# Deeper rings for the attention probabilities in a latent-attention and feed-forward layer, with a new hand-written order

## The reference

```
x = x + layernorm(attention(layernorm(x)))
x = x + layernorm(ffn(layernorm(x)))
```

## Time and profile before

| | us |
|---|---|
| median of 3 runs | 1710.68 (1709.68 to 1716.02) |
| the profiled execution, its own time | 1718.1 |
| its span, first to last instruction | 1716.3 |
| TensorE / VectorE / ScalarE / GpSimd busy | 1572.2 / 1147.7 / 1069.0 / 952.9 |
| DMA queue q1, share of 16 engines | 72.0% |
| mean granted TensorE clock | 0.980 |

### The profile page before, as it was taken

The page is one execution under the profiler, slowest core; times in us unless marked ns, Lnnn a source line. Parts: engine busy times, 40 slices in busy tenths (PEclk is TensorE's granted clock), DMA queues, the critical chain, the costliest instruction groups (busy, mean ns, idle before and its releaser), DMA issues.

```text
span 1716.3 us, 30452 instructions
## 1 busy us (share of the span) xinstructions
PE 1572.2 (92%) x10720; PEld 1275.9 (74%) x10720; DVE 1147.7 (67%) x2548; ACT 1069.0 (62%) x2159; POOL 952.9 (56%) x911
## 2 busy tenths in 40 slices
PE   5878999999998999998999999999978899999997
PEld 5856777778777777777877777777766677888775
DVE  6866677777777777776777777777766542323356
ACT  5677777777777777777877777777754433212122
POOL 2556677677676677676767677677622321111132
PEclk9899999999999999999999999999998999999998
DMA  8669999998999989899889898988996300201022
GB/s 280 227 140 206 164 200 181 189 200 174 203 175 190 180 190 201 184 187 188 171 172 190 164 179 169 183 171 165 184 186 239 121 25 1 74 1 39 1 92 80
DMA packets 661095, 268.84 MB, mean 157 GB/s; under 512 B 608432, under 2 KB 619184, under 8 KB 658768
## 3 DMA queue, kind: packets, MB, share of 16 engines
q1 hardware_dynamic: 660944, 266.90, 72.0%
HBM read 69.70 MB, written 29.36 MB: 58 GB/s over the span
## 4 chain that ended last, share of the span: by engine, by line
PE 56%; DMA 14%; DVE 11%; ACT 6%; POOL 6%; issue 4%; SPq 2%; POOLq 0%; ACTq 0%; DVEq 0%
PE f_ps L116 14%; PE s_ps L973 12%; PE x_ps L116 11%; DMA pt<-pk 10%; PE o_ps L987 9%; PE fd_ps L116 6%; DMA qs<-q_raw 3%; DVE pk L1384 3%; PE x_ps L996 2%; DVE s_ps L1371 1%; POOL q_low L1561 1%; POOL qf L1554 1%; POOL qs L1551 1%; SPq L772 1%; ACT ot_high L1194 1%
## 5 line engine op out<-in xcount | busy, mean ns | idle before, releaser
L1384 DVE SCALAR_TENSOR_TENSOR pk<-s_ps,pk 128x256 f16<-128x256 f32 (+7 forms) x512 | 383.7, 749 | 132.7 <-ACT pk L1176 132.4
L1168 ACT ACTIVATE s_ps<-s_ps,nbias 128x256 f32<-128x256 f32 (+7 forms) x512 | 371.3, 725 | 129.7 <-DVE nbias L1371 126.2
L1371 DVE CUSTOM_DVE_ANT_0 s_ps<-s_ps,far_sb 128x256 f32<-128x256 f32 (+7 forms) x512 | 388.4, 759 | 36.1 <-PE s_ps L973 30.9
L987 PEld LDWEIGHTS o_ps<-lat,pt 128*128 128x128 f16 x4608 | 268.2, 98 | 137.7 <-issue 70.4
L1176 ACT ACTIVATE pk<-s_ps 128x256 f16<-128x256 f32 (+7 forms) x512 | 339.6, 663 | 34.1 <-DMA pt<-pk 28.4
L987 PE MATMUL o_ps<-lat,pt 128*128 128x130 f16 x4608 | 312.0, 221 | 51.6 <-DMA pt<-pk 41.9
L1551 POOL TENSOR_TENSOR qs<-qs,sin_q 64x512 f32<-64x512 f32 x128 | 164.4, 1284 | 224.7 <-DMA qs<-q_raw 217.9
L973 PE MATMUL s_ps<-k_high,q_high 128*128 128x512 f32 (+3 forms) x768 | 283.6, 369 | 5.0 <-DVE k_low L1351 2.0
L973 PE MATMUL s_ps<-k_low,q_high 128*128 128x512 f32 (+3 forms) x768 | 257.1, 347 | 0.0
L1599 POOL TENSOR_TENSOR mid_low<-mid,mid_high 128x512 fp32r<-128x512 f32 (+1 forms) x44 | 57.2, 1300 | 303.1 <-ACT mid_high L1265 303.1
L973 PE MATMUL s_ps<-k_high,q_low 128*128 128x512 f32 (+3 forms) x768 | 224.3, 346 | 0.0
(11 more groups left out here) (134 smaller groups left out, 2622.1 us busy)
## 6 DMA issues: line engine op xcount, KB each, us to landing
weff_in<-weff SPq DMA_DIRECT2D x64, 256.0 KB, 3.2
qs<-q_raw SPq DMA_DIRECT2D x256, 64.0 KB, 2.1
weff<-weff_sb SPq DMA_DIRECT2D x8, 1024.0 KB, 5.3
wo_sb<-wo SPq DMA_DIRECT2D x16, 512.0 KB, 4.5
m_fold<-m_in SPq DMA_DIRECT2D x8, 1024.0 KB, 6.9
m_in<-m_fold SPq DMA_DIRECT2D x8, 1024.0 KB, 6.2
xin<-x SPq DMA_DIRECT2D x16, 256.0 KB, 4.7
wqn_sb<-wqn SPq DMA_DIRECT2D x8, 512.0 KB, 6.9
```

The source lines that it names most:

```text
L987: ins = e.matmul(M.o_ps[:, i % 2, :], M.pt[:, u % NPT, m, :], M.lat2[:, b * JT + (m - blocks[0]) // 2, :], start=m == blocks[0], stop=m == ...
L1168: e.activation(M.scores_of(i), M.scores_of(i), ACT.Exp, bias=M.nbias[:, i % 4:i % 4 + 1], scale=-1.0).then_inc(S.exp)
L1371: e.tensor_tensor_reduce(out=s, in0=s, in1=M.far_sb[:, SEQ - width:SEQ], scale=1.0, scalar=3e38, op0=ALU.add, op1=ALU.min, accum_out=M.nbi ...
L1384: e.scalar_tensor_tensor(out=M.halves_of(i)[:, :, 1, :], in0=M.tiles_of(i), scalar=P_SCALE, in1=M.halves_of(i)[:, :, 0, :], op0=ALU.mult, ...
```

## The change

The ring of pk gets four slots (was three) and that of pt five (was four); the semaphores of the transposes go by NPK. VALUES puts each product two steps later. All other offsets of the attention order, the tile order, the start and pace of the early feed-forward pieces and PACES are new. In the prologue, the two operations that split wa leave `latents_begin` and become turns of their own, so that VectorE's wa_low stands behind the statistics of the first tile.

```diff
-NX, NA, NPK, NPT, NON = 4, 3, 3, 4, 8
+NX, NA, NPK, NPT, NON = 4, 3, 4, 5, 8
-AFTER_SCORES = dict(minimum=1.02, exponential=1.16, split_high=1.78, split_low=2.94)
-TURN_PROBS = 2.41
-VALUES = 6.09
-AFTER_VALUES = dict(invert_sums=1.31, outputs_norm=1.68, outputs_add=3.17)
-TURN_STEPS = (4.75, 4.72)
-AFTER_TURN = dict(outputs_high=0.0, outputs_low=0.96)
-Q_STEPS = (0.0, 2.66)
-AFTER_QUERIES = dict(queries_raw=0.69, queries_swap=0.03, queries_turn=1.93)
-O_STEPS = (4.97, 7.03)
-AFTER_OUTPUT = dict(output_add=0.36, output_store=1.5)
-FOLD_STEP = 1.07
-AFTER_FOLD = dict(fold_high=0.02, fold_low=1.08, fold_store=1.5)
-END_STEP, END_EVERY = 9.71, 1.38
+AFTER_SCORES = dict(minimum=0.5, exponential=1.59, split_high=2.17, split_low=3.36)
+TURN_PROBS = 3.23
+VALUES = 8.07
+AFTER_VALUES = dict(invert_sums=1.39, outputs_norm=1.27, outputs_add=2.37)
+TURN_STEPS = (6.7, 4.29)
+AFTER_TURN = dict(outputs_high=0.02, outputs_low=0.64)
+Q_STEPS = (0.0, 2.37)
+AFTER_QUERIES = dict(queries_raw=0.36, queries_swap=0.0, queries_turn=2.53)
+O_STEPS = (4.27, 6.91)
+AFTER_OUTPUT = dict(output_add=1.14, output_store=1.5)
+FOLD_STEP = 1.01
+AFTER_FOLD = dict(fold_high=0.13, fold_low=1.34, fold_store=1.5)
+END_STEP, END_EVERY = 13.73, 1.73
-EARLY_START, EARLY_EVERY = 6.94, 0.84
-PACES = (7, 3, 4)
+WEIGHT_STEPS = (-0.5, 0.5)
+EARLY_START, EARLY_EVERY = 8.94, 1.19
+PACES = (5, 3, 3)
-TILES = (1, 6, 4, 3, 0, 7, 5, 2)
+TILES = (3, 4, 6, 1, 2, 5, 7, 0)
 def prologue_order():
+    at(WEIGHT_STEPS[0], "weights_round")
+    at(WEIGHT_STEPS[1], "weights_rest")
 def scalar_program(e, M, S):
-    def latents_begin():
+    def weights_round():
         w.wait_ge(S.wa_in, DMA)
         e.activation(M.wa_high[:, :, :], M.wa_raw[:, :, :], ACT.Copy).then_inc(S.wa_high)
 def vector_program(e, M, S):
         e.memset(M.eps1[:, 2:3], RMS_EPS / L_SCALE ** 2).then_inc(S.eps)
+
+    def weights_rest():
         w.wait_ge(S.wa_high, 1)
         e.tensor_tensor(M.wa_low[:, :, :], M.wa_raw[:, :, :], f32(M.wa_high[:, :, :]),
                         ALU.subtract).then_inc(S.wa_low)
```

More of the change, by code:

```diff
@@ L1274, in down @@
         e.activation(M.acc_of(i), M.d_ps[DOWN[g, i] % 2][:, :], ACT.Copy).then_inc(S.part_first)
-    run(dict(latents_begin=latents_begin, deviation=deviation, x_high=x_high,
+    run(dict(weights_round=weights_round, deviation=deviation, x_high=x_high,
              squares=squares, norm_queries=norm_queries, latents_high=latents_high,
@@ L1496, in finish @@
                 e.tensor_tensor(M.acc_of(i), M.acc_of(i), M.xin_of(i), ALU.add).then_inc(S.y_dve)
-    run(dict(latents_begin=latents_begin, statistics=statistics, normalise=normalise, x_low=x_low,
+    run(dict(latents_begin=latents_begin, weights_rest=weights_rest, statistics=statistics, normalise=normalise, x_low=x_low,
              norm_keys=norm_keys, latents_low=latents_low, weights_low=weights_low, latents_over=latents_over,
```

## The result

| | before | after |
|---|---|---|
| median of 20 runs each, us | 1714.30 (1709.68 to 1716.20) | 1718.96 (1712.85 to 1723.97) |
| ratio, 95% interval | | 1.0027 [1.0017, 1.0037] |
| span of the profiled execution, us | 1716.3 | 1718.0 |
| mean granted TensorE clock | 0.980 | 0.978 |

A forecast was written before the change was run, and what follows sets the result against it. TensorE, 92% busy, was taken to lead, with waits for turned probabilities the largest. -35 (slots, distance) +22 (x_ps) +1.5 (folds) -0.6 (beginning) made -12.1 us: 1699 against the median of 1710.68, range 1676 to 1711.

The forecast's parts named there:

- Step (1): Attention, more slots and distance for turned probabilities: TensorE's waits for pt go, -35 us, bounds -42 and -12.
- Rival C: DMA engines and SP's queue set the pace, transposes come no faster whatever the slots: 1710 us, 20%.
- Step (2): Order on the x_ps bank: less lost before queries (-10.8), new waits of output products after a turn (+33); net +22 us.
- The queries' part: Queries waiting for x_ps behind the turn at 9.77: 0.4 us lost instead of 0.76, 30 times, -10.8 us; wait halved.
- Step (3): Other orders in attention, on SP, GpSimd, ScalarE and VectorE: operations moved past each other cost nothing.
- The queries' "nothing": GpSimd's queries_turn 0.6 step later costs nothing, queries being due 15 us after; without that cover 1.3 us a head.
- The part on the exponential: ScalarE's outputs_high ahead of an exponential makes it wait for the turn: nothing; if the cover is gone, 0.5 us each.
- Step (4): Beginning: VectorE's statistics of tile 0 ahead of wa_low, xn 0.6 us earlier: -0.6 us, bounds 0 and -1.1.
- Step (5): End of attention 0, bounds -5 and +5 us; PACES in the feed-forward 0, bounds -2 and +3.
- The PACES part: Feed-forward side work spread wider: 0 us, bounds -2 and +3.
- Rival D: VectorE's split_low behind a row minimum makes scores wait for their bank, deciding from 13 us: slower, 1731 us, 15%.
- The sum: Whole kernel: -35+22+1.5-0.6 = -12.1 us, so 1699 against the median; as rival A 45%, own range 1688 to 1706.

The follow-up runs named there:

- the best kernel: The changed kernel with PACES (7, 3, 4), the m_in load behind the queries' swap and the second turn of outputs ahead of the products: 0.9833 of before, 1687.07 us.
- PACES and load: The changed kernel with PACES back at (7, 3, 4) and the m_in load behind the queries' swap: 0.9872 of before, 26.6 us below after.

## Why the prediction was wrong

**Step (1), "-35", failed by its size.** The removal of the waits came as forecast: that of products on pt went to 0.2 us (below 8 was the sign) and ScalarE's wait on pk, 28.2, is gone. But slots and distance alone are worth 10 us, less than the lower bound of 12. The step took a wait as its own price: 30.9 us of waiting for pt, so 30.9 us to gain. The wait was where a nearly full resource showed. In the 1100 us from 150 to 1250, the issues in the timeline of SP's queue add up to 957 us before (transposes 748, swaps 142, other loads and stores 67) and to 983 after; in the best kernel to 1003, and with half transposes to 557 and 564. With the wait for pt gone the next client in that queue was late: the weights of the queries in the unchanged order (21.0 us), the swap when the transposes went earlier in the new one (70.0, 77.4), pt again when they went later (33.0). Each of these moves put the wait elsewhere and lost time; halving the transposes took some 50 us off both kernels. Rival C named the resource, and gave it the wrong strength: something was gained (10 us), not nothing. My argument against it was the window at a DMA share of 1.04 with TensorE at 48.51 of 50 us. One window in which all clients happened to be in time says nothing of those in which they aren't. The prediction also misapplied the Trainium skill ("Perfetto Trace Analysis", Identifying the Most-Contended Engine). The section says to judge TensorE by its weight loads, which gave 0.77, but for DMA it wants the use of HBM and not the engines' occupancy, since 16 engines make occupancy misleading. So it doesn't name the DMA engines by their share of 0.92; the HBM traffic in the page of the profile is 58 GB/s. That transposes held the kernel back rests on the halved ones alone.

**Step (2), "+22", was right in its places and too high in time.** The wait of the output product after a turn is 0.89 us long as in the row above; in the table it is 30.2 us for both kinds together, of which some 24 are the 29 or 30 new ones once the 5.7 that remain without it are taken off. 1.1 us was forecast for each, +33 in time, 28 in the table. The queries' part more than halved, from 13.1 to 5.7, as forecast. Taking the new wait away gave 8.7 us in time (6.7 on top of PACES and load), because the turn then waited for the queries' copy. By these runs a wait on x_ps is worth only what the next user of the bank doesn't wait for instead.

**Step (3), "nothing", failed, and cost 15 us.** I listed what each queue's operations were moved past and looked for the swap only against the transposes. The load of m_in hangs on an offset of another family, `O_STEPS[1] + 1`: 8.03 before, level with the swap at 8.03 and behind it, and 7.91 after, ahead of the swap at 8.0. Lowering O_STEPS[1] by 0.12 carried it past. The queries' "nothing" failed too: scores waited 12.9 us for q_low, 20.8 in the best kernel. The place of queries_turn on GpSimd isn't to blame, since the wait left the table with the second swap one transpose earlier and with half transposes. The part on the exponential stands: no wait of TensorE goes back to one.

**Step (4), "-0.6"**, agrees with what could be measured. The first xn starts 2.4 us after wa_low in after and 3.2 before, which makes 0.8; the rest of the way from 12.7 to 11.4 us is that wa_low itself started 0.4 earlier. The first scores came at 93.5 to 96.7 us in the runs with the new prologue and at 95.2 to 96.4 in those with the old one, so the 2.3 us between the two profiled executions are for the most part their scatter.

**Step (5), end and PACES, "0".** The end gained 5.6 us, just outside +-5, in one execution each. The PACES part, bounded by +3, cost 10. TensorE busy 371 of 396 us was read as "nothing waits for side work"; the edit delays the side work itself, so the rows of before could not show it. The question should have been when each piece is due.

**Rival D** (15%): its wait is 2.7 us, below the 13 at which it decides. It appeared, with 48.5 us, when the additions were moved by 0.93 steps, some 2.1 us. So the place was rightly seen; how wide its margin is, 0.6 us or another, isn't shown.

**The sum.** The forecast counted from the median of three runs, 1710.68; that of 20 is 1714.30, so 3.6 of the 20 us between 1699 and 1718.96 are the starting point. By scores alone, distance (-12.6 in its trace), x_ps (+8.6) and load (+17.7) make +13.7, and +0.5 was seen. So some 13 us seem to be gained by other offsets of the new order, from single executions with a scatter of up to 4 us each and as if the parts added up. It is in line with after being 5.4 us faster than before with half transposes, although PACES costs it 10. Which offsets did it stays open.

## What to carry to other kernels

A removed wait pays in full only if nothing else is served by what was late. Before pricing it, add up the occupancy of the queue behind it (0.87 here) and ask which of its other clients is next. Halving the suspected resource's work, with all other work as it is, tells in one run about what the resource costs.

In an order made of offsets, print each queue's sequence before and after and compare all neighbours, above all large loads against small transfers that something waits for; 0.12 of a step cost 15 us here. And an operation whose place hangs on another's moves with it: an output product 0.9 steps later cost 34 us through its addition, and an addition 0.92 steps too late on GpSimd over 200.

## What the runs showed of the hardware that I had not expected

A transposing DMA of one pair (18 blocks of 128x128 halves) holds SP's queue 3.02 us in the median and up to 6.7, where the two transfers of a swap together hold it 1.16 and the 1 MB load 0.53. Half the transpose holds it 1.32 and lands after 3.4 us instead of 5.0. So the long holding comes with the transpose's size, while the landing shrinks by less than half. The holding isn't the transpose's own work alone: directly behind the eight 1 MB loads and swaps of after it was 4.3 to 5.7 us.

A 1 MB load issued 0.62 us ahead of the queries' swap (two transfers of 64 KB) made it take 6.9 us, by the copy that it released, against 2.1 in the median; the load itself lands after 7.0 us. In all eight places the small transfers waited for the large one in front, and in the run with the load behind them they didn't.
